# Where the row maximum of the attention scores leaves them, and in what order four engines take their steps

## The reference

```python
h = group_norm(x, gn_scale, gn_bias)              # 32 groups
q, k, v = nin(h, Wq, bq), nin(h, Wk, bk), nin(h, Wv, bv)
w = einsum('bchw,bcHW->bhwHW', q, k) * C ** -0.5  # per batch 1024 x 1024 scores
w = softmax(w, axis=-1)
x = x + nin(einsum(w, v), Wp, bp)                 # block 1
t = to_tokens(x)
t = t + linear_attention(layer_norm(t))           # block 2: softmax over the keys, 4 heads of 32
t = t + moe(layer_norm(t))                        # block 3: router, best 2 of 8 experts, gelu
out = from_tokens(t)
```

## Time and profile before

| | |
|---|---|
| median of 3 runs | 338.52 us (337.98 to 339.28) |
| time of the profiled execution | 337.77 us |
| its span (first to last instruction) | 336.0 us |
| mean granted TensorE clock | 0.989 |
| busy: PE, DVE, ACT, POOL | 303.2, 254.6, 189.7, 102.6 us |

### The profile page before, as it was taken

How to read it: one execution, slowest core, us unless ns; L and a number is a source line. 1 busy time by engine, 2 the same in 40 slices (tenths; PEclk the granted TensorE clock), 3 DMA queues, 4 the chain that set the end, 5 groups by cost and what they waited for, 6 DMA issues and landing times.

```text
span 336.0 us, 5110 instructions
## 1 busy us (share of the span) xinstructions
PE 303.2 (90%) x1569; PEld 237.8 (71%) x1569; DVE 254.6 (76%) x591; ACT 189.7 (56%) x330; POOL 102.6 (31%) x154
## 2 busy tenths in 40 slices
PE   2798979979989889878988997999999997999996
PEld 2677758957878777666877785877767775666884
DVE  4999577577487598978689777787688685776995
ACT  1357464657560577346277666358567444856883
POOL 2464440059201754600446200089120037000000
PEclk9999999989999999999999999999999997999999
DMA  6702000010000011000000106386420692239501
GB/s 180 268 1 64 0 1 2 0 65 0 0 0 3 0 64 52 12 13 0 0 1 0 62 12 190 139 373 244 165 104 0 227 341 86 71 101 390 194 30 63
DMA packets 12757, 29.58 MB, mean 88 GB/s; under 512 B 2192, under 2 KB 5952, under 8 KB 10816
## 3 DMA queue, kind: packets, MB, share of 16 engines
q1 hardware_dynamic: 11872, 29.00, 24.5%
q10 hardware_dynamic: 864, 0.33, 0.4%
HBM read 24.73 MB, written 4.59 MB: 87 GB/s over the span
## 4 chain that ended last, share of the span: by engine, by line
PE 62%; DVE 23%; ACT 6%; issue 5%; POOL 2%; DMA 1%; DVEq 0%; POOLq 0%
PE ring L1379 7%; PE ring L1381 7%; PE ring L1380 7%; PE ring L1682 7%; PE ring L1394 7%; PE scores L1379 6%; PE scores L1381 6%; PE scores L1380 6%; DVE row_max L998 5%; DVE pT_lo L1004 4%; ACT prob L667 2%; PE ring L1531 2%; DVE lst L1034 2%; PE ring L1496 2%; ACT pT_hi L673 1%
## 5 line engine op out<-in xcount | busy, mean ns | idle before, releaser
L798 ACT ACTIVATE gel<-scores,b_c 128x512 f32<-128x512 f32 x64 | 43.9, 688 | 35.7 <-PE scores L1381 32.8
L1004 DVE TENSOR_TENSOR pT_lo<-ring,pT_hi 128x512 fp32r<-128x512 f32 x64 | 40.9, 680 | 15.3 <-ACT pT_hi L673 14.9
L998 DVE TENSOR_REDUCE row_max<-scores 128x1 f32<-128x1024 f32 x32 | 38.8, 1212 | 10.8 <-PE scores L1381 10.7
L667 ACT ACTIVATE prob<-scores,row_max 128x1024 f32<-128x1024 f32 x32 | 35.8, 1118 | 17.1 <-DVE row_max L998 17.0
L553 POOL TENSOR_SCALAR rstd<-lmv 128x8 f32<-128x8 f32 x8 | 2.1, 259 | 138.6 <-DVE lmv L1040 138.6
L673 ACT ACTIVATE pT_hi<-ring 128x512 fp32r<-128x512 f32 x64 | 35.0, 597 | 14.4 <-PE ring L1394 14.4
L1394 PE MATMUL ring<-ident,prob 128*128 128x128 f32 x256 | 35.3, 280 | 7.9 <-ACT prob L667 3.5
L1394 PEld LDWEIGHTS ring<-ident,prob 128*128 128x128 f32 x256 | 29.4, 143 | 12.9 <-ACT prob L667 4.5
L1379 PE MATMUL scores<-wT_hi,w_hi 128*128 128x512 f32 x64 | 34.4, 538 | 0.0
L1379 PE MATMUL scores<-k_both,q_hi 128*128 128x512 f32 x64 | 27.5, 429 | 1.0 <-DVE k_both L988 1.0
L1379 PE MATMUL ring<-pT_hi,v_hi 128*128 128x512 f32 x64 | 26.7, 417 | 1.2 <-DVE pT_lo L1004 1.2
(11 more groups left out here) (296 smaller groups left out, 721.0 us busy)
## 6 DMA issues: line engine op xcount, KB each, us to landing
pT_hi<-scratch_s SPq DMA_DIRECT2D x8, 1024.0 KB, 7.1
prob<-scratch_s SPq DMA_DIRECT2D x4, 1024.0 KB, 8.1
k_both<-scratch_s SPq DMA_DIRECT2D x3, 1024.0 KB, 5.7
z_in<-scratch_z SPq DMA_DIRECT2D x8, 256.0 KB, 2.9
out_dram<-out_s SPq DMA_DIRECT2D x8, 256.0 KB, 2.1
xb<-in_x_dram SPq DMA_DIRECT2D x3, 512.0 KB, 3.2
scratch_z<-out_s SPq DMA_DIRECT2D x2, 512.0 KB, 2.8
k_both<-scratch_s SPq DMA_DIRECT2D x4, 256.0 KB, 4.8
```

Of the source, the lines that this page charges most:

```text
L667: act.activation(prob[:, i % 2, :], scores[:, 2 * (i % 2):2 * (i % 2) + 2, :].rearrange("p a t -> p (a t)"), ACT.Exp, bias=row_max[:, i:i ...
L798: act.activation(half(gel, s % 2), scores[:, s % 2, :], ACT.Gelu, bias=b1_c[:, s % E:s % E + 1]).then_inc(e_gelu, 1)
L998: dve.tensor_reduce(row_max[:, i:i + 1], scores[:, 2 * (i % 2):2 * (i % 2) + 2, :].rearrange("p a t -> p (a t)"), AX.X, ALU.max, negate=Tr ...
L1004: dve.tensor_tensor(tile_group(pT_lo, n, i), as_tiles(ps(place, unit)), tile_group(pT_hi, n, i).bitcast(FP32), ALU.subtract).then_inc(drai ...
```

## The change

1. **The maximum.** DVE's pass over the scores becomes a `tensor_scalar` that multiplies by -1, writes all 1024 values to `prob[:, i % 2]` in SBUF and gives their minimum (the negated maximum) by its accumulator output. ACT's exponential reads and writes `prob` in place, with scale -1. S(i) now waits on `s_max` (tile i-2 copied out) where it waited on `s_exp`. Before the pass DVE waits that T(i-2) has been read.
2. **Order, batches 1 to 3.** T5 moves ahead of S6 on PE, ahead of max(6) on DVE, and ahead of p and exp(6) on ACT. exp(1) moves on ACT behind v0, v1 and T0. The banks come from tables; each unit has the bank that the rotation gave, but for the places that T5, p and c exchange.
3. **Batch 0** has lists of its own (`opening_batch`). ACT: T5 ahead of exp(6). PE and DVE keep their order; DVE has `first_norm` twice.
4. **Setup.** ACT makes `h_hi` (`split_first`), DVE no longer does and makes `h_lo` earlier; the four bias columns are loaded by SP's queue, behind wk and ahead of wv.

```diff
             sp.dma_start(wk_raw, wk).then_inc(ld_w["wk"], 16)
+            for i, v in enumerate((bq, bk, bv, bp)):
+                sp.dma_start(cols[:, i:i + 1], v.rearrange("(c a) -> c a", a=1)).then_inc(ld_w["cols"], 16)
             sp.dma_start(wv_s[:, :], wv).then_inc(ld_w["wv"], 16)
...
+            def split_first():
+                for n in range(HALVES):
+                    act.wait_ge(ld_x0b if n else ld_x[0], 16)
+                    act.activation(half(h_hi, n), half(xb, n), ACT.Copy).then_inc(h_hi_made, 1)
...
                 act.wait_ge(s_max, b * TILES + i + 1)
-                act.activation(prob[:, i % 2, :], scores[:, 2 * (i % 2):2 * (i % 2) + 2, :].rearrange("p a t -> p (a t)"),
-                               ACT.Exp, bias=row_max[:, i:i + 1], accum_out=row_sum[:, 0, i:i + 1]).then_inc(s_exp, 1)
+                act.activation(prob[:, i % 2, :], prob[:, i % 2, :], ACT.Exp, bias=row_max[:, i:i + 1], scale=-1.0,
+                               accum_out=row_sum[:, 0, i:i + 1]).then_inc(s_exp, 1)
...
             channel_means(0, 1)
-            high_first(0)
+            low_first(0)
             group_deviation(SETUP, 0, 1)
-            high_first(1)
+            low_first(1)
             group_variance(SETUP, 0, 1)
-            low_first(0)
-            low_first(1)
             first_weights()
             first_norm()
...
-            def row_maximum(b, i):
+            def row_maximum(place, b, i):
+                if i >= 2:
+                    wait_filled(dve, place, f"T{i - 2}b")
+                elif place is not FIRST:
+                    wait_filled(dve, place, f"T{TILES - 2 + i}b")
                 dve.wait_ge(s_made, b * TILES + i + 1)
-                dve.tensor_reduce(row_max[:, i:i + 1], scores[:, 2 * (i % 2):2 * (i % 2) + 2, :].rearrange("p a t -> p (a t)"),
-                                  AX.X, ALU.max, negate=True).then_inc(s_max, 1)
+                dve.tensor_scalar(prob[:, i % 2, :],
+                                  scores[:, 2 * (i % 2):2 * (i % 2) + 2, :].rearrange("p a t -> p (a t)"),
+                                  -1.0, None, ALU.mult, ALU.min, accum_out=row_max[:, i:i + 1]).then_inc(s_max, 1)
...
             def score(b, i):
                 if not (isinstance(b, int) and b == 0 and i < 2):
-                    pe.wait_ge(s_exp, b * TILES + i - 1)
+                    pe.wait_ge(s_max, b * TILES + i - 1)
...
                 if first_batch(m) and s < 2:
-                    pe.wait_ge(s_exp, B * TILES)
+                    pe.wait_ge(s_max, B * TILES)
...
+                  T4b=1, T5a=2, T5b=3, p0=0, p1=1, c0=2, c1=3, g=0, OT0=1)
...
```

More of the change, by code:

```diff
@@ L110, in earlier, with placed @@
         return self.before[bank] + n
+def placed(banks, before):
+    count, found = list(before), {}
+    for unit, bank in banks.items():
+        found[unit] = (bank, count[bank] - before[bank])
+        count[bank] += 1
+    return Place(found, before), count
 def place_of(units, before, first=0, wide=None):
@@ L1162, in w_halves, with opening_batch @@
                 return [w[:, bass.ds(lb * T + n * BANK, BANK)] for n in range(HALVES)]
+            def opening_batch(place, b):
+                project(place, b, "q0", q_hi, q_lo, bqs_c)
+                project(place, b, "k0", k_hi, k_lo, bk_c)
+                project(place, b, "k1", k_hi, k_lo, bk_c)
+                project(place, b, "q1", q_hi, q_lo, bqs_c)
+                take(place, "wvT", wvT[:, :])
+                first_norm()
+                group_stats(1)
+                row_maximum(place, b, 0)
+                merge_weights()
+                row_maximum(place, b, 1)
+                group_stats(2)
+                project_v(place, b)
+                turn_probs(place, b, 0)
+                row_maximum(place, b, 2)
+                setup_rest()
+                turn_probs(place, b, 1)
+                group_stats(3)
+                channel_means(1, B - 1)
+                row_maximum(place, b, 3)
+                turn_probs(place, b, 2)
+                row_maximum(place, b, 4)
+                group_deviation(place, 1, B - 1)
+                turn_probs(place, b, 3)
+                row_maximum(place, b, 5)
+                group_variance(place, 1, B - 1)
+                invert_sums(b, 0)
+                group_affine(2, 1, B - 1)
+                weights_again()
+                turn_probs(place, b, 4)
+                row_maximum(place, b, 6)
+                turn_probs(place, b, 5)
+                row_maximum(place, b, 7)
+                dve.wait_ge(experts_split, 3)
+                residual(place, b, 0)
             def batch(place, b, la, lc):
@@ L1179, in batch @@
                 project(place, b, "q1", q_hi, q_lo, bqs_c)
-                if la is None:
-                    take(place, "wvT", wvT[:, :])
-                if la is not None:
-                    invert_sums(la, 1)
+                invert_sums(la, 1)
                 if lc is not None:
-                    for n in range(HALVES):
-                        take_out(place, lc, n)
-                    for n in range(HALVES):
-                        norm2_stats(place, lc, n)
-                if la is None:
-                    group_stats(1)
@@ L1563, in turn_comb, with opening_batch @@
                 turn(place, "c1", [comb[:, 1, :]])
+            def opening_batch(place, b):
+                project(place, b, "q0", wq_hi, wq_lo)
+                project(place, b, "k0", wk_hi, wk_lo)
+                project(place, b, "k1", wk_hi, wk_lo)
+                project(place, b, "q1", wq_hi, wq_lo)
+                pe.wait_ge(ld_w["wv"], 16)
+                turn(place, "wvT", [wv_s[:, :]])
+                for unit in ("q0", "k0", "k1"):
+                    wait_drained(pe, place, unit)
+                score(b, 0)
+                wait_drained(pe, place, "wvT")
+                pe.wait_ge(ld_w["wp"], 16)
+                small(place, "wpv", C, wvT[:, :], wp_s[:, :])
+                pe.wait_ge(ld_w["cols"], 64)
+                small(place, "bias_o", 1, wp_s[:, :], bv_c)
+                score(b, 1)
+                wait_drained(pe, place, "wpv")
+                pe.wait_ge(h_f_made, 1)
+                project_v(place)
+                turn_probs(place, b, 0)
+                score(b, 2)
+                pe.wait_ge(ld_w["qkv"], 16)
+                turn(place, "l1qT", [wqkv_s[:, 0:C]])
+                pe.wait_ge(ld_w["rows8"], 32)
+                turn(place, "rowsT", [rows8[:, 0, :], rows8[:, 1, :]], rows=E, step=E)
+                turn_probs(place, b, 1)
+                turn_x(place, b)
+                score(b, 3)
+                turn_probs(place, b, 2)
+                wait_drained(pe, place, "q1")
+                score(b, 4)
+                group_means(place, 2, 1, B - 1)
+                turn_probs(place, b, 3)
+                score(b, 5)
+                group_variances(place, 2, 1, B - 1)
+                attend(place, 0, 0, 2)
+                attend(place, 0, 2, 4)
+                attend(place, 0, 4, 6)
+                attend(place, 0, 6, TILES)
+                turn_probs(place, b, 4)
+                score(b, 6)
+                turn_probs(place, b, 5)
+                score(b, 7)
+                turn_o(place, 0)
             def batch(place, b, la, lc):
[L1566 to L1567 removed]
+                turn_probs(place, la, 6)
                 if lc is not None:
@@ L1618, in batch @@
                 if lc is not None:
-                    for n in range(HALVES):
-                        turn_w(place, lc, n)
+                    turn_w(place, lc, 0)
+                    turn_w(place, lc, 1)
                 turn_probs(place, b, 2)
```

258 lines of the change are left out of this document (106 added, 152 removed).

## The result

The changed kernel takes 334.21 us (median of 4 executions, 333.55 to 335.48), the kernel before 338.50 (4 executions, 337.98 to 339.28): ratio 0.9876, 95% interval 0.9837 to 0.9915. It is 4.3 us faster, and the forecast of 337.1, with its range down to 334.8, missed it.

A forecast was written before the change was run, and what follows sets the result against it. It took PE as the bound, and DVE where PE waits for a ring bank. Its terms summed to -1.4 us on the profiled 337.77, so 336.4, or 337.1 us as a median; range 334.8 to 340.6.

The forecast's parts named there:

- pass and exponential: Maxima and exponentials on the path: 12 passes at +0.07 us (+0.84) and six exponentials from SBUF at +0.03 (+0.2).
- second h_f: DVE writes h_f again ahead of max(0) of batch 0, not covered: +0.8 us (0.4 to 2.1).
- setup: Start of the kernel: DVE loses two casts but still waits for PE's group mean and GpSimd's power: 0.
- end of batch 0: T5's copies ahead of exp(6) on ACT, PE no longer waits for T6b's bank: -1.2 us (0.6 to 1.3).
- v first: Batch 1, v's copies ahead of exp(1) on ACT, so v_lo starts earlier: -0.65 us (0.5 to 0.7).
- clock behind that wait: Batch 1, 73 to 76 us: without PE's 2.09 us wait the clock stays up: -1.1 us, all or nothing.
- end of batch 1: max(7) and residual 0.7 us earlier, but exp(7) still holds T7; 0.2 to 0.45 left: -0.3 us.
- batches 2 and 3: v first gives nothing, and at the end T7 follows exp(7) as before: 0 (-0.3 to +0.6 us).
- The early release: S(i+2) waits for max(i) in place of exp(i), but stands behind T's on PE anyway: worth nothing.
- T7 of batch 0: Sign in the changed profile: T7 of batch 0 starts at 50.2 us.
- the faster one: Rival: DVE's gain at the batch ends, or a GpSimd/DVE shift at 131 to 144 us, comes through: 335.1 us, chance 0.20.
- the slower one: Rival: copying pass longer than the reduction at 12 maxima, deciding from 0.26 us a pass: 340.5 or 341.6 us, chance 0.16.

The follow-up runs named there:

- pass_alone: The kernel before with the new pass alone (copy and minimum in one, exponential in place, scores released by s_max), old orders and banks: 338.81 us, ratio 1.0014.
- one_norm: The changed kernel without the second writing of h_f in batch 0: 334.28 us, ratio 0.9869.
- setup_alone: The kernel before with the new setup alone: 336.81 us, ratio 0.9949.
- setup_old: The changed kernel with the setup as before (DVE's casts and late low parts, bias columns asked for by ACT): 337.20 us, ratio 0.9958.
- end0_old: The changed kernel with exp(6) ahead of T5's copies on ACT in batch 0 alone, as before: 336.30 us, ratio 0.9955.
- exp1_first: The changed kernel with exp(1) ahead of v's copies on ACT in batches 1 to 3, as before: 335.84 us, ratio 0.9923.
- ends_old: The changed kernel with the old order at the end of batches 1 to 3 on PE, ACT, DVE and in the banks: 334.79 us, ratio 0.9913.
- early_share: The changed kernel with SP asking for the experts' first shares ahead of the routed rows: 333.76 us, ratio 0.9881.
- low_beside: The changed kernel with two more DVE subtractions where the old setup made h's low parts: 336.50 us, ratio 0.9930.
- delayed: The changed kernel with gmul computed five times in a row in place of once: 336.32 us, ratio 0.9907.
- filled_wait: The kernel before with six more matmuls in PE's 2.09 us wait in batch 1, between S3 and T2: 338.36 us, ratio 1.0006.
- orders_alone: The changed kernel with the old pass (reduction in PSUM, scores held until the exponential), new orders, banks and setup kept: 334.07 us, ratio 0.9891.
- best: The changed kernel with one h_f writing, the experts' first shares asked for early, and six more matmuls in PE's w_n wait: 332.84 us, ratio 0.9841.

## Why the prediction was wrong

| term | forecast | measured | from |
|---|---|---|---|
| pass and exponential | +1.04 | +0.8 (old lists) | pass_alone, trace |
| second h_f | +0.8 | +0.8 | one_norm, trace |
| setup | 0 | -0.72 directly, -2.0 to -3.0 in all | setup_alone, setup_old |
| end of batch 0 | -1.2 | -1.24 | end0_old, trace |
| v first | -0.65 | -0.85 | exp1_first, trace |
| clock behind that wait | -1.1 | -0.97, where it falls | exp1_first, trace |
| end of batch 1 | -0.3 | -0.6 | ends_old, trace; net of the 0.33 of the pass it is -0.24 (T2 to q0: 23.39 against 24.60 - 0.97) |
| batches 2 and 3 | 0 | -0.5, at the end of batch 2 | q0 to q0: 55.68 against 56.20; q0 to PV1 in batch 3: 56.23 against 56.16 |
| load of the shares | not in it | +0.45 | early_share, trace |

With the setup at -0.72 the measured terms add up to -2.8. The spans are 3.07 apart; in no row are the 0.62 us of slow start against the changed kernel (last section) and the 0.72 of the second fall, at 281 us, against the kernel before, which leaves 0.1. So in the traces the sum of -1.4 was too small by 1.4, and half of that is the setup; in the medians the setup weighs more:

- **The step that failed is "The setup: 0".** It said that DVE "then waited for PE's group mean and for GpSimd's power, and still will". DVE does still wait for the power. But I took the power's duration as given, and it was the low parts of DVE beside it that made it long; the prediction priced the removed casts and never asked what the moved low parts had been running beside. By medians this term alone carries the miss: without the new setup the changed kernel is at 337.20 (setup_old), 1.3 below the kernel before, and my other terms together had been -1.4.
- **How 0.72 becomes 2 to 3 us** is only partly settled. One part is fewer falls of the clock: the kernel before has a mean clock of 0.995 or less in 70 of 70 executions, setup_old in 11 of 12; the kernels with the new setup, the new lists and no wait of PE of 2 us (eight of them and the changed kernel) were above it in 34 of 51. A fall costs 0.97 at 73 us, 1.58 at 51 (end0_old, T7 to T1: 17.98 in place of 16.40), 1.60 at 145 (setup_old, 142.90 to 151.77 in place of 142.05 to 149.32) and 0.72 at 281. But falls are not all of it. At a mean clock of 0.993 to 0.995 the median is 338.2 for the kernel before (44 executions) and 336.6 for setup_alone (8), so 1.6 us are won with as many falls. At 0.998 or more low_beside takes 334.50 to 337.39 (6 executions) and delayed 336.35 to 336.47 (3), the changed kernel 333.55 to 334.79 (3). A second part is the slow start of PE (last section), which the mean clock doesn't hold: from gmul to the first S it is 6.6 to 6.8 us in ten of the 17 traces and 7.4 to 7.8 in seven, and the three longest, 7.56, 7.68 and 7.84, are those with a late gmul (pass_alone, setup_old, and delayed from its fifth gmul), though three others with a late gmul started fast. What picks the slow start and the place of a fall stays open, and with it how often a late gmul meets them.
- **The clock term** had the right size for one fall (0.97 to 1.04 against 1.1) and the wrong idea of it. I treated the fall at 73 us, seen in one execution, as a property of that wait, all or nothing. It is one of several places; filled_wait shows that removing this one changes nothing by itself.
- **The pass** was right in sum and wrong in its parts: no 0.07 at each maximum, but 0.33 us at the end of batch 1 and 0.23 in batch 0. In the new lists the traces put it at 0.6, and the medians of orders_alone and the changed kernel can't be told apart.
- **The end of batch 1** was mis-sized: I let 0.2 to 0.45 of the 0.7 through, and 0.6 came.
- **The ends of batches 2 and 3** fell short by 0.5, all of it in batch 2, since I named the wrong bound. I watched exp(7) holding T7. In batch 2, q0 stands ahead of T7 on PE and waited for DVE's residual, 0.98 us at 152.22, now 0.46 at 149.32; DVE reaches the residual earlier as it no longer idles for T5. No run separates this from the rest of the change.
- **The early release** and **T7 of batch 0** came as forecast.
- Of the **rivals**, the faster one (335.1) was nearest, and for the most part by luck: it had a contention of GpSimd and DVE in it, but at 131 to 144 us and not in the setup; right was its other half, that the gain at the end of batch 1 comes through. (In the slower one the border of 0.26 a pass should be 0.24: (340.2 - 338.2) / 12 + 0.07.) What carried the miss lay where the forecast had looked least, in the first 10 us and in one execution's clock.
- The forecast moved from the profiled execution to the median as if both kernels stood alike to theirs; they stood 1.3 us apart.

## What to carry to other kernels

When a step is moved off an engine, ask what it ran beside, not only what stood behind it: a short GpSimd step on the path can be made long by a DVE pass with two SBUF inputs that nobody waits for. Before a stretch of low clock in one profile gets a price, look at the mean clock of every execution; if it differs from one to the next, the price is a frequency times a cost, and only timing shows it. And compare executions at a like clock too: what differs there has another cause. And when a stage moves forward, follow the loads that are asked for on another queue behind it: here one that had been hidden took 0.45 us back, and 0.75 more from the next improvement.

## What the runs showed of the hardware that I had not expected

- At the start PE runs slowly for a time that differs, and the row of the granted clock doesn't show it: it says 1.00 from 5 us on in all these traces. The same matmuls of 512 columns, k's first projection, in the changed kernel and in best:

```profile
12.53 0.63 PE L1403 MATMUL ring<-h_hi,wk_hi 128*128 128x512 f32 x1
12.96 0.63 PE L1404 MATMUL ring<-h_lo,wk_hi 128*128 128x512 f32 x1
...
13.81 0.41 PE L1403 MATMUL ring<-h_hi,wk_hi 128*128 128x512 f32 x1
```

```profile
12.10 0.40 PE L1403 MATMUL ring<-h_hi,wk_hi 128*128 128x512 f32 x1
12.34 0.39 PE L1404 MATMUL ring<-h_lo,wk_hi 128*128 128x512 f32 x1
```

  gmul starts at 9.00 and 9.02 in the two, the first S at 16.40 and 15.78: 0.62 us that goes with the slow start, seen in seven of the 17 traces. It hid the gain of the setup when I compared the first S of the two kernels (16.48 and 16.40), since the execution of before had started fast and the one of after slowly.
- GpSimd's first step, a TENSOR_SCALAR on one value per partition, went from 0.19 to 0.56 us and its power from 0.57 to 0.89 beside DVE's subtractions. In each of the five traces the first step ended 0.04 to 0.05 us behind DVE's first subtraction (8.71 and 8.66 in the kernel before).
- The second instruction that reads DVE's accumulator takes 83 ns and lies under the next one.
